# Half chunks: skipping the second half of a tile's last gathered chunk in four of five graph layers

## Chip, cores and metric

The kernel runs on one core of one Trainium2 chip. The metric is device time in microseconds (us) of one launch, and lower is better. TensorE multiplies matrices, VectorE (DVE in the rows) and ScalarE (ACT) work on elements, GpSimd (POOL) issues the indirect DMAs that gather and scatter rows of a table in memory, SyncE (SP) issues plain DMAs. Each engine runs an instruction stream of its own, and the streams meet at semaphores.

## The reference

A graph with 3125 nodes and 103125 directed edges (every node has an edge to itself) goes through four blocks, each followed by a layer norm of input plus output. Block 0 is attention over the incoming edges with 8 heads, block 1 a relational layer, block 2 two graph attention layers (GAT, 8 heads and then 1), block 3 a graph attention layer with 4 heads beside a selective scan over the nodes. All but block 1 have the same core; here is the one of block 2:

```python
e = jax.nn.leaky_relu(el[src] + er[dst], 0.2)
m = jax.ops.segment_max(e, dst, num_segments=n)
ex = jnp.exp(e - m[dst])
ssum = jax.ops.segment_sum(ex, dst, num_segments=n)
a = ex / ssum[dst]
rst = jax.ops.segment_sum(feat[src] * a[..., None], dst, num_segments=n)
```

For every edge the row `feat[src]` must be fetched, weighted and added to the row of its destination. A node has between 1 and 58 incoming edges.

## The kernel before

The nodes are sorted by their number of incoming edges, from most to fewest, and cut into T = 25 tiles of 128, one node per partition. A tile's edges are worked in **chunks** of S = 8 slots: slot s of a chunk holds for each of the 128 nodes the row of one neighbour (256 numbers and the heads' terms). So a tile needs as many chunks as its largest node fills: 8, 6, 6 for tiles 0 to 2, 5 for tiles 3 to 12, 4 for tiles 13 to 22, and 3 for the last two, 116 in a layer. A slot that a node doesn't fill carries an index beyond the table, which the gather leaves out, and an `extras` value that takes it out of the softmax. From the inputs, the largest nodes of tiles 0, 1, 2, 7 to 12 and 19 to 22 (13 tiles) fill at most the first four slots of their tile's last chunk.

`edge_softmax` works the layers conv (block 0), GAT 1 and GAT 2; `attend_and_scan` works the last one (its names begin with `m_`) with the selective scan on VectorE between its chunks. In all of them, per chunk:
1. SP (`load_record`) waits until buffer b has been gathered before, and loads the next 8 x 128 indices into `index[b]`; after `released[b]` it loads `extras[b]`.
2. POOL (`gather`) waits for the indices and for `released[b]`, and issues 8 indirect DMAs, one per slot, each adding 16 to the semaphore `gathered[b]`.
3. VectorE (`logits`) waits for `gathered[b]`, makes the logits and a running maximum; ScalarE takes the exponential; VectorE (`weigh`) multiplies rows and probabilities (L1100), which releases the buffer, and sums over slots, by itself in GAT and with TensorE in conv and the last layer.

Chunks alternate between the buffers b = 0 and b = 1 (a pair), and an odd last chunk has a third one, `TAIL_BUF`. In the last layer a tile's first two chunks have buffers of their own: `FIRST_BUF` and `SECOND`; there are four in all, and `SECOND` and the tail chunk take turns in one. The number of pairs is not known when the program is built: every engine reads words of a small table `sched` into registers at a tile's start (`Visit` in `edge_softmax`, `Stay` in `attend_and_scan`; a `value_load`), and the loop over pairs and the branch for the tail are done by registers. `fetch_nodes` makes the table once from the largest in-degree of each tile (`first`), by small VectorE operations on one partition. A tile's first two chunks are written out, with the previous tile's end (normalising, layer norm, scatter of its rows by POOL between the two gathers) woven in. The helper `new_steps` counts VectorE's finished operations: `st.do` appends one that waits for all before it.

What a wait compares with is worked out from the registers. Before, a chunk always adds 8 x 16:

```python
v.wait_ge(gathered[b], 16 + (u + 1) * 16 * S)
```

where `u = w.uses(a, b)` is how often buffer b has been used by then. The 16 comes from a small DMA that primes each semaphore.

Of the kernel before, what the change touches and what calls it, by code (L numbers as in the profile page):

```python
# [14 lines left out]
I32 = mybir.dt.int32  # L15
# [362 lines left out]
def fetch_nodes(nc, io, dr, kp, pr):  # L378


    with ExitStack() as ctx:
# [10 lines left out]
        more, cum_more, all_records = sb("f_more", [1, T]), sb("f_cummore", [1, T]), sb("f_allrecords", [1, T])  # L392
        has_more, long_tiles = sb("f_hasmore", [1, T]), sb("f_longtiles", [1, 1])
# [33 lines left out]
        def _(v):  # L427
# [27 lines left out]
            st.do(v.tensor_copy(kp["sched"][:, COUNT, 0:T], per[:, 0, :]))  # L455
            for k in (CHUNKS, RECORDS, USES):
# [345 lines left out]
CHUNKS, RECORDS, USES, COUNT, CODE, TAILS, LATER, LATER_CODE, MORE, MORE_AT, WORD = range(11)  # L802
# [6 lines left out]
TAIL_BUF = 2  # L809


class Visit:


    def __init__(self, eng, kp, t):
# [12 lines left out]
        self.chunks_end = self.chunks + count  # L828

# [8 lines left out]
FIRST_BUF, SECOND = 3, 4  # L838


class Stay:


    def __init__(self, eng, kp, t):
        def read(row, least, most):
            return eng.value_load(kp["sched"][0:1, row, bass.ds(t, 1)], min_val=least, max_val=most)
        code = read(LATER_CODE, 0, (CHUNKS_MAX // 2 << TAIL_BITS) + T)
        later = read(LATER, 0, E // S + 2)
# [4 lines left out]
        self.chunks = self.later + self.records + t  # L853

# [34 lines left out]
def visit(eng, kp, t, chunk, in_first=None):  # L889

    w = Visit(eng, kp, t)
# [12 lines left out]
    return w  # L904


def edge_layer(nc, io, dr, kp, layer):
# [10 lines left out]
    with ExitStack() as ctx:  # L918
# [60 lines left out]
        def _(sp):  # L979
# [8 lines left out]
            def load_record(w, a, b):  # L988
# [4 lines left out]
                sp.wait_ge(gathered[b], 16 + u * 16 * S)  # L993
# [6 lines left out]
            visit(sp, kp, 0, load_record)  # L1000
            with tile_loop(nc, sp, 1, T) as t:
                visit(sp, kp, t, load_record)

        @block.gpsimd
        def _(pool):
# [6 lines left out]
            def gather(w, a, b):  # L1012
# [7 lines left out]
                for s in range(S):  # L1020
# [3 lines left out]
                        bounds_check=limit, oob_is_err=False).then_inc(gathered[b], 16)  # L1024

# [20 lines left out]
            for t in range(2):  # L1046
                visit(pool, kp, t, gather)
            with tile_loop(nc, pool, 2, T) as t:
                visit(pool, kp, t, gather, first_pair(t - 2))
# [6 lines left out]
        def _(v):  # L1056
# [136 lines left out]
            def tile(t, first):  # L1193
                w = Visit(v, kp, t)
# [605 lines left out]
def attend_and_scan(nc, io, dr, kp):  # L1800
# [5 lines left out]
    with ExitStack() as ctx:  # L1806
# [82 lines left out]
        def _(sp):  # L1889
# [8 lines left out]
            def load_record(w, j, b):  # L1898
# [6 lines left out]
                sp.wait_ge(gathered[b], 16 + n * 16 * S)  # L1905
# [6 lines left out]
            with tile_loop(nc, sp, 0, T) as t:  # L1912
                w = Stay(sp, kp, t)
# [5 lines left out]
        def _(pool):  # L1919
# [5 lines left out]
            def gather(w, j, b):  # L1925
# [7 lines left out]
                for s in range(S):  # L1933
# [4 lines left out]

            with tile_loop(nc, pool, 0, T) as t:
                w = Stay(pool, kp, t)  # L1940
# [154 lines left out]
        def _(v):  # L2095
# [108 lines left out]
            def logits(st, w, j, b):  # L2204

                n = w.uses(j, b)
                v.wait_ge(gathered[b], 16 + (n + 1) * 16 * S)
# [38 lines left out]
            def tile(t, front, ahead, before):  # L2246
                w = Stay(v, kp, t)
# [280 lines left out]
def network(nc, io, result):  # L2528
# [17 lines left out]
    with ExitStack() as ctx:  # L2546
        def sb(name, shape, dt=F32):
# [5 lines left out]
            "inv_deg": sb("inv", [P, T]), "sched": sb("sched", [1, 11, 32], I32), "ident": sb("ident", [P, P]),  # L2553
# [55 lines left out]
```

## Time and profile before

| | us |
|---|---|
| median of 3 runs | 8107.87 (8107.5 to 8110.19) |
| the profiled execution's own time | 8107.49 |
| its span in the trace | 8105.7 |

| layer | from, to | chunks | gathers |
|---|---|---|---|
| conv | 430, 1810 | 116 | 928 |
| relational (not changed) | 1810, 3254 | 116 | 928 |
| GAT 1 | 3254, 4545 | 116 | 928 |
| GAT 2 | 4545, 5864 | 116 | 928 |
| last, with the scan | 5864, 7600 | 116 | 928 |

The share of busy time is an average over layers with different limits. In a timeline row, the number in brackets is the engine's idle time just before the instruction, and the name behind the arrow is what the trace holds for the event that ended it. An instruction on registers, a branch and a semaphore instruction are not counted as busy: they show as idle time, and the arrow then names whatever came last before.

### The profile page before, as it was taken

To read this page: it belongs to the slowest core of one execution; us is meant where nothing else is said; L and a number is where in the kernel's file an instruction comes from. 1 tells how busy PE (TensorE), PEld (TensorE's weight loads), DVE (VectorE), ACT (ScalarE), POOL (GpSimd) and SP (SyncE) were. 2 spreads that over 40 slices of the span, in tenths; PEclk is the share of its full clock that TensorE was granted. 3 is DMA by queue.
4 is the path that set the end of the run, shared out by engine and by line. 5 is a ranking of instruction groups with operands and counts; after the bars stand their busy time and mean duration, and the time that the engine had idled before them with its cause. 6 is when DMAs were issued, how large, how long until landed. Compare 5 with 4: busy or idle time off the path is not lost. (4 is left out here: it accounts for less than half of the span.)

```text
span 8105.7 us, 73810 instructions
## 1 busy us (share of the span) xinstructions
PE 3327.5 (41%) x15180; PEld 2657.1 (33%) x15181; DVE 5585.2 (69%) x11215; ACT 1258.9 (16%) x2734; POOL 5360.7 (66%) x4985
## 2 busy tenths in 40 slices
PE   3444544445667766112222100000155555555444
PEld 3233333334666666011111000000044444444333
DVE  7578888883333434788888677777767887777444
ACT  4101111110111111000000000010122232223111
POOL 0666766666777776777777677777667777776301
PEclk7767676777888888555555555555577777777666
DMA  2345555542332322333333233333233333332100
GB/s 82 91 133 166 166 156 165 157 125 82 89 86 82 88 84 59 88 95 92 91 100 88 59 91 94 87 96 91 71 92 107 108 104 101 107 99 81 51 6 9
DMA packets 489231, 773.98 MB, mean 95 GB/s; under 512 B 298796, under 2 KB 319767, under 8 KB 485436
## 3 DMA queue, kind: packets, MB, share of 16 engines
q0 software_dynamic: 265920, 667.09, 29.6%
q10 hardware_dynamic: 20536, 77.34, 2.5%
q1 hardware_dynamic: 202688, 28.69, 2.3%
q14 instruction: 68, 0.56, 0.0%
q8 instruction: 19, 0.31, 0.0%
HBM read 823.08 MB, written 46.52 MB: 107 GB/s over the span
## 5 line engine op out<-in xcount | busy, mean ns | idle before, releaser
L1021 POOL DMA_INDIRECT gat_rows<-scratch_gat,gat_index x1856 | 1858.3, 1001 | 583.7 <-issue 545.1
L1934 POOL DMA_INDIRECT m_rows<-scratch_gat,m_index x928 | 1219.7, 1314 | 507.0 <-issue 272.9
L1467 POOL DMA_INDIRECT rel_rows<-scratch_x,rel_index x928 | 1016.3, 1095 | 295.4 <-issue 281.8
L1021 POOL DMA_INDIRECT conv_rows<-scratch_kv,conv_index x928 | 931.5, 1004 | 420.8 <-issue 253.8
L1317 PE MATMUL conv_ps<-conv_work,k_ident 128*128 128x256 f32 x1856 | 680.9, 546 | 748.9 <-DVE conv_work L1100 678.2
L724 PE MATMUL gat_ps<-k_ident,gat_cur 128*128 128x128 f32 x100 | 34.4, 448 | 2127.9 <-DVEq L1184 1201.4
L1317 PEld LDWEIGHTS conv_ps<-conv_work,k_ident 128*128 128x128 f32 x1856 | 520.4, 287 | 909.8 <-issue 719.9
L724 PEld LDWEIGHTS gat_ps<-k_ident,gat_cur 128*128 128x128 f32 x100 | 14.4, 203 | 2163.5 <-DVEq L1184 1219.7
L1732 PE MATMUL rel_ps<-rel_factor,rel_rows 128*128 128x128 f32 x3712 | 595.8, 336 | 274.8 <-DMA rel_rows<-scratch_x,rel_index 274.3
L1732 PEld LDWEIGHTS rel_ps<-rel_factor,rel_rows 128*128 128x128 f32 x3712 | 577.9, 249 | 287.2 <-DMA rel_rows<-scratch_x,rel_index 183.7
L1112 DVE TENSOR_REDUCE gat_red<-gat_work 128x256 f32<-128x2048 f32 x182 | 652.2, 3583 | 0.0
L1100 DVE TENSOR_TENSOR gat_work<-gat_rows,gat_psprob 128x2048 f32<-128x2048 f32 x232 | 530.5, 2287 | 61.9 <-ACT gat_psprob L1252 50.4
L1990 PE MATMUL m_ps<-m_work,k_ident 128*128 128x256 f32 x1664 | 494.6, 466 | 171.4 <-DVE m_work L2224 171.4
L1990 PEld LDWEIGHTS m_ps<-m_work,k_ident 128*128 128x128 f32 x1664 | 392.6, 241 | 261.9 <-issue 190.0
L1974 PE MATMUL m_ps<-m_hs,k_ident 128*128 128x128 f32 x1600 | 278.8, 355 | 320.3 <-DVEq L2193 320.3
L1974 PEld LDWEIGHTS m_ps<-m_hs,k_ident 128*128 128x128 f32 x1600 | 269.3, 267 | 335.1 <-DVEq L2193 335.1
L1252 ACT ACTIVATE gat_psprob<-gat_logit 128x72 f32<-128x72 f32 (+1 forms) x232 | 48.2, 208 | 2129.9 <-DVE gat_logit L1092 2129.9
L2368 POOL DMA_INDIRECT out_x<-j_o,j_node x25 | 36.6, 1465 | 434.0 <-DVEq L2493 427.9
L1083 DVE TENSOR_TENSOR conv_dots<-conv_rows,conv_psown 128x2048 f32<-128x2048 f32 x116 | 265.3, 2287 | 83.5 <-DMA conv_rows<-scratch_kv,conv_index 37.7
L2224 DVE TENSOR_TENSOR m_work<-m_rows,m_ps 128x2048 f32<-128x2048 f32 x104 | 237.9, 2287 | 80.5 <-ACT m_ps L2056 80.5
L1100 DVE TENSOR_TENSOR conv_work<-conv_rows,conv_psprob 128x2048 f32<-128x2048 f32 x116 | 265.1, 2285 | 21.4 <-ACT conv_psprob L1252 20.4
L1084 DVE TENSOR_REDUCE conv_logit<-conv_dots 128x64 f32<-128x2048 f32 x116 | 265.1, 2286 | 4.0
(488 smaller groups left out, 7568.2 us busy)
## 6 DMA issues: line engine op xcount, KB each, us to landing
m_bc<-scratch_bc ACTq DMA_DIRECT2D x25, 2048.0 KB, 8.7
gat_rows<-scratch_gat,gat_index POOLq DMA_INDIRECT x1856
conv_rows<-scratch_kv,conv_index POOLq DMA_INDIRECT x928
rel_rows<-scratch_x,rel_index POOLq DMA_INDIRECT x928
m_rows<-scratch_gat,m_index POOLq DMA_INDIRECT x928
scratch_runs<-e_runs_sb ACTq DMA_DIRECT2D x1, 6453.1 KB
scratch_runs<-e_runs_sb SPq DMA_DIRECT2D x1, 6437.5 KB
scratch_kv<-p_row ACTq DMA_DIRECT2D x25, 256.0 KB, 2.5
```

What stands on the lines that cost most here:

```text
L1021: pool.indirect_dma_start(out=rows[b][:, s, :], out_offset=None, in_=table, in_offset=bass.IndirectOffsetOnAxis(ap=index[b][:, s:s + 1], a ...
L1083: st.do(v.tensor_tensor(dots[:], rows[b][:, :, 0:F], over_slots(own[:], S), ALU.mult))
L1084: st.do(v.tensor_reduce(lg, dots[:].rearrange(per_head, h=H), X, ALU.add))
L1100: v.tensor_tensor(work[b][:].rearrange(per_head, h=H), rows[b][:, :, values:values + F].rearrange(per_head, h=H), over_dims(prob[:, 0:S, : ...
L1112: st.add(v.tensor_reduce(red[:], slots, X, ALU.add))
L1317: ins = pe.matmul(ps_sum[min(b, 1)], ident, work[b][:, s, :], start=s == 0, stop=s == S - 1)
L1467: pool.indirect_dma_start(out=rows[b][:, g, :], out_offset=None, in_=dr["x1"], in_offset=bass.IndirectOffsetOnAxis(ap=index[b][:, g:g + 1] ...
L1732: ins = pe.matmul(ps_sums[h * 2 + g // 4][:, (g % 4) * P:(g % 4 + 1) * P], rows[b][:, g, h * P:(h + 1) * P], factor[b][:, g * BASES:(g + 1 ...
L1934: pool.indirect_dma_start(out=rows[b][:, s, :], out_offset=None, in_=dr["gat3"], in_offset=bass.IndirectOffsetOnAxis(ap=index[b][:, s:s + ...
L1974: ins = pe.matmul(ps_y[:, k, :], kp["ident"][:], hs[:, k, n, :], start=n == 0, stop=n == NS - 1)
L1990: ins = pe.matmul(ps_sum[bank_of(b)], kp["ident"][:], work[b][:, s, :], start=s == 0, stop=s == S - 1)
L2224: v.tensor_tensor(work[b].rearrange(per_head, h=H), rows[b][:, :, 0:F].rearrange(per_head, h=H), over_dims(prob[:, 0:S, :], D), ALU.mult). ...
```

## The change

`fetch_nodes` works out for each tile whether its last chunk is needed as a whole (the tile has three chunks or more, and its largest node fills more than `8 * count - 4` slots), and sums this up over the tiles before. The result is two new rows of `sched`, `WHOLE` and `LATER_WHOLE`, in one word per tile: the flag of this tile, how many tail chunks before were whole, how many b = 1 chunks before were whole. POOL gathers slots 4 to 7 of a b = 1 or tail chunk inside a branch on `whole_now`. Because a buffer's semaphore then no longer grows by 128 with each use, everyone who waits for it (SP in `load_record`, VectorE in `logits`) computes the value in halves of 64. In the relational layer `halves` stays off. What the skipped slots would have held stays in the buffer from an earlier chunk, and `extras` takes them out as before. VectorE still works on all eight slots.

```diff
@@ fetch_nodes
             st.do(v.tensor_copy(kp["sched"][:, COUNT, 0:T], per[:, 0, :]))
+            st.add(v.tensor_scalar(free[:], per[:, 0, :], float(S), float(-S // 2), ALU.mult, ALU.add))
+            st.add(v.tensor_scalar(half[:, 0, :], per[:, 0, :], 3.0, None, ALU.is_ge))
+            st.do(v.tensor_tensor(half[:, 1, :], per[:, 1, :], per[:, 2, :], ALU.subtract))
+            st.do(v.tensor_tensor(free[:], free[:], first[:], ALU.is_ge))
...
+            for k in range(2):
+                st.do(v.tensor_tensor_scan(wholes[:, k, :], whole[:, k, :], zero[:], 0.0, ALU.add, ALU.add))
+                st.do(v.tensor_tensor(wholes[:, k, :], wholes[:, k, :], whole[:, k, :], ALU.subtract))
...
+            st.add(v.tensor_copy(kp["sched"][:, WHOLE, 0:T], half[:, 0, :]))
+            st.do(v.scalar_tensor_tensor(half[:, 0, :], tile_no[:], -64.0, half[:, 0, :], ALU.mult, ALU.add))
+            st.do(v.tensor_scalar(kp["sched"][:, LATER_WHOLE, 0:T], half[:, 0, :], 64.0, None, ALU.add))
@@ new
+HALF = 16 * (S // 2)
+class Halves:
+    def read_halves(self, read, row, t):
+        word = read(row, t, 0, (CHUNKS_MAX // 2 << 6) + 63)
+        self.last_whole, self.whole_tails, self.whole_pairs = word & 1, (word >> 1) & 31, word >> 6
+
+    def whole_now(self, j, b):
+
+        if b == TAIL_BUF:
+            return self.last_whole
+        return (self.pairs > j + 1) | self.last_whole | self.tail
+
+    def landed_before(self, j, b):
+        if not self.halves or b not in (1, TAIL_BUF, SECOND):
+            return self.uses(j, b) * (2 * HALF)
+        return self.uses(j, b) * HALF + (self.whole_pairs + j if b == 1 else self.whole_tails + self.firsts(b)) * HALF
+
+    def landed(self, j, b):
+        if not self.halves or b not in (1, TAIL_BUF, SECOND):
+            return (self.uses(j, b) + 1) * (2 * HALF)
+        now = 1 if b == SECOND else self.whole_now(j, b)
+        return self.landed_before(j, b) + HALF + now * HALF
+
+def gather_slots(pool, w, j, b, one):
+    for s in range(S // 2):
+        one(s)
+    if b not in (1, TAIL_BUF):
+        for s in range(S // 2, S):
+            one(s)
+        return
+    with pool.If(w.whole_now(j, b) > 0):
+        for s in range(S // 2, S):
+            one(s)
@@ Visit and Stay, __init__
+        self.halves = halves
+        if halves:
+            self.read_halves(read, WHOLE, t)
@@ load_record, in both kinds of layer
-                sp.wait_ge(gathered[b], 16 + u * 16 * S)
+                sp.wait_ge(gathered[b], 16 + w.landed_before(a, b))
@@ gather, in both
-                for s in range(S):
+                def one(s):
                     pool.indirect_dma_start(
...
+                gather_slots(pool, w, a, b, one)
@@ logits, in both
-                v.wait_ge(gathered[b], 16 + (u + 1) * 16 * S)
+                v.wait_ge(gathered[b], 16 + w.landed(a, b))
@@ tile of edge_softmax
-                w = Visit(v, kp, t)
+                w = Visit(v, kp, t, halves=True)
```

How the engines' instruction lists change. `ISA` rows are register moves, address arithmetic or semaphore instructions, `TENSOR_LOAD` is a read of the table into a register. First VectorE in GAT 2, from the tile loop's head to the first operation on the first chunk. Before:

```order
L1237 ISA
L817 TENSOR_LOAD k_sched
L817 ISA x2
L68 ISA
L1196 MEMSET gat_top 128x1
L1197 ISA
L1197 COPY gat_own<-k_er 128x1
L1079 ISA
L1086 TENSOR_TENSOR gat_logit<-gat_rows,gat_own 128x8
```

And in the changed kernel:

```order
L1314 ISA
L881 TENSOR_LOAD k_sched
L881 ISA x3
L881 TENSOR_LOAD k_sched
L881 ISA x2
L68 ISA
L1273 MEMSET gat_top 128x1
L1274 ISA
L1274 COPY gat_own<-k_er 128x1
L1156 ISA
L1157 REGISTER_ALU
L1163 TENSOR_TENSOR gat_logit<-gat_rows,gat_own 128x8
```

There is a second read of the table, with three more `ISA` rows, ahead of the memset. Next VectorE in the same tile at its second chunk (b = 1), from the last operations of the previous tile's end to the first on the chunk. Before:

```order
L1163 COPY gat_node<-k_info 128x1
L755 RECIPROCAL gat_small<-gat_small 128x1
L756 TENSOR_SCALAR gat_cur<-gat_out,gat_small 128x256
L1086 TENSOR_TENSOR gat_logit<-gat_rows,gat_own 128x8
```

And in the changed kernel:

```order
L1240 COPY gat_node<-k_info 128x1
L776 RECIPROCAL gat_small<-gat_small 128x1
L777 TENSOR_SCALAR gat_cur<-gat_out,gat_small 128x256
L1156 ISA
L1156 REGISTER_ALU
L1156 ISA
L1156 REGISTER_ALU x4
L1156 ISA
L1163 TENSOR_TENSOR gat_logit<-gat_rows,gat_own 128x8
```

Eight instructions on registers now stand between the two operations, where there was none. Last POOL in GAT 2's loop over the remaining pairs and the tail chunk behind it. Before:

```order
L899 ISA
L1021 DMA gat_rows<-scratch_gat,gat_index 128x257 x16
L899 REGISTER_ALU
L899 COMPARE_AND_BRANCH
L898 UNCONDITIONAL_BRANCH
L902 REGISTER_ALU
L902 COMPARE_AND_BRANCH
L1015 REGISTER_ALU
L1015 ISA
L1021 DMA gat_rows<-scratch_gat,gat_index 128x257 x8
```

And in the changed kernel:

```order
L974 ISA
L1096 DMA gat_rows<-scratch_gat,gat_index 128x257 x12
L871 ISA
L871 REGISTER_ALU x2
L871 COMPARE_AND_BRANCH
L1096 DMA gat_rows<-scratch_gat,gat_index 128x257 x4
L871 UNCONDITIONAL_BRANCH
L974 REGISTER_ALU
L974 COMPARE_AND_BRANCH
```

The sixteen gathers of a pair are now twelve and, behind a compare and branch, four.

## Rows read from the trace of the kernel before

A page's group (rows 3) has: line, engine, operation, tiles, count, then busy us, mean ns of one, idle before and what ended most of it. A window (rows 2) has: from and to, length, then busy us and number of instructions of PE, PEld, DVE, ACT and POOL, then TensorE's granted clock as a share of full speed, the share of DMA time, GB/s. A timeline row has: start, duration, engine, line, operation, tiles, and the idle before in brackets. In rows 1 PE is TensorE's multiplying and PEld its loading of weights.

**Rows 1.** The page: busy time, share of the span and instructions of each engine.
```profile
PE 3327.5 (41%) x15180; PEld 2657.1 (33%) x15181; DVE 5585.2 (69%) x11215; ACT 1258.9 (16%) x2734; POOL 5360.7 (66%) x4985
```

**Rows 2.** The windows view: conv, GAT 1, GAT 2, last layer.
```profile
430.00:1810.00 1380.00, 666.43 (x1815) 509.49 (x1816) 1172.56 (x2113) 222.38 (x337) 955.17 (x951) 0.70 0.57 156
...
3254.00:4545.00 1291.00, 287.11 (x600) 160.83 (x600) 1035.92 (x2005) 66.26 (x244) 956.70 (x957) 0.52 0.34 88
4545.00:5864.00 1319.00, 72.56 (x159) 38.39 (x160) 1013.99 (x2102) 118.62 (x294) 981.40 (x982) 0.50 0.33 87
5864.00:7600.00 1736.00, 960.86 (x4199) 807.06 (x4198) 1320.36 (x2824) 488.77 (x1200) 1223.02 (x932) 0.76 0.33 97
```

**Rows 3.** The page's costliest groups: gathers of both GAT layers, and the last's.
```profile
L1021 POOL DMA_INDIRECT gat_rows<-scratch_gat,gat_index x1856 | 1858.3, 1001 | 583.7 <-issue 545.1
L1934 POOL DMA_INDIRECT m_rows<-scratch_gat,m_index x928 | 1219.7, 1314 | 507.0 <-issue 272.9
```

**Rows 4.** Timeline of POOL in GAT 2, one gather.
```profile
5098.49 0.99 POOL L1021 DMA_INDIRECT gat_rows<-scratch_gat,gat_index  x1 [0.30 <-issue]
```

**Rows 5.** Timeline of VectorE in GAT 2, tile 9 and the next memset.
```profile
5100.11 0.06 DVE L1196 MEMSET gat_top<- 128x1 f32 x1 [1.43 <-DVE gat_den L1127]
...
5101.33 0.17 DVE L1086 TENSOR_TENSOR gat_logit<-gat_rows,gat_own 128x8 f32<-128x8 f32 x1 [0.97 <-DMA gat_rows<-scratch_gat,gat_index]
...
5104.11 0.48 DVE L1155 SCALAR_TENSOR_TENSOR gat_out<-k_a,k_inv,gat_out 128x256 f32<-128x256 f32 x1 [0.17 <-DVE gat_out L1154]
...
5114.48 0.17 DVE L1086 TENSOR_TENSOR gat_logit<-gat_rows,gat_own 128x8 f32<-128x8 f32 x1 [0.79 <-DMA gat_rows<-scratch_gat,gat_index]
...
5124.90 0.17 DVE L1086 TENSOR_TENSOR gat_logit<-gat_rows,gat_own 128x8 f32<-128x8 f32 x1 [1.96 <-DMA gat_rows<-scratch_gat,gat_index]
...
5135.28 0.17 DVE L1086 TENSOR_TENSOR gat_logit<-gat_rows,gat_own 128x8 f32<-128x8 f32 x1 [1.92 <-DMA gat_rows<-scratch_gat,gat_index]
...
5145.00 0.17 DVE L1086 TENSOR_TENSOR gat_logit<-gat_rows,gat_own 128x8 f32<-128x8 f32 x1 [1.22 <-DMA gat_rows<-scratch_gat,gat_index]
...
5154.93 0.06 DVE L1196 MEMSET gat_top<- 128x1 f32 x1 [1.44 <-DVE gat_den L1127]
```

**Rows 6.** Timeline of VectorE in GAT 1: tile 9 (three rows), tile 20, tile 21's start.
```profile
3821.60 0.22 DVE L1086 TENSOR_TENSOR gat_logit<-gat_rows,gat_own 128x64 f32<-128x64 f32 x1 [1.32 <-DMA gat_rows<-scratch_gat,gat_index]
...
3832.01 0.23 DVE L1086 TENSOR_TENSOR gat_logit<-gat_rows,gat_own 128x64 f32<-128x64 f32 x1 [1.45 <-DMA gat_rows<-scratch_gat,gat_index]
...
3841.74 0.22 DVE L1086 TENSOR_TENSOR gat_logit<-gat_rows,gat_own 128x64 f32<-128x64 f32 x1 [0.76 <-DMA gat_rows<-scratch_gat,gat_index]
...
4328.22 0.23 DVE L1086 TENSOR_TENSOR gat_logit<-gat_rows,gat_own 128x64 f32<-128x64 f32 x1 [0.23 <-DVE gat_hid L1190]
...
4338.01 0.23 DVE L1086 TENSOR_TENSOR gat_logit<-gat_rows,gat_own 128x64 f32<-128x64 f32 x1 [0.83 <-DMA gat_rows<-scratch_gat,gat_index]
...
4347.70 0.23 DVE L1086 TENSOR_TENSOR gat_logit<-gat_rows,gat_own 128x64 f32<-128x64 f32 x1 [0.76 <-DMA gat_rows<-scratch_gat,gat_index]
...
4359.28 0.22 DVE L1086 TENSOR_TENSOR gat_logit<-gat_rows,gat_own 128x64 f32<-128x64 f32 x1 [0.45 <-DVE gat_own L1197]
```

**Rows 7.** Timelines in conv: POOL and VectorE in tile 9, VectorE in tile 16.
```profile
1039.46 1.00 POOL L1021 DMA_INDIRECT conv_rows<-scratch_kv,conv_index  x1 [5.30 <-DVE conv_work L1100]
...
1064.82 2.29 DVE L1083 TENSOR_TENSOR conv_dots<-conv_rows,conv_psown 128x2048 f32<-128x2048 f32 x1 [0.32 <-DVE conv_den L1127]
...
1421.97 2.29 DVE L1083 TENSOR_TENSOR conv_dots<-conv_rows,conv_psown 128x2048 f32<-128x2048 f32 x1 [0.82 <-DMA conv_rows<-scratch_kv,conv_index]
```

**Rows 8.** Timeline of VectorE in the last layer: a chunk of tile 1, the start of tile 10.
```profile
6058.32 0.19 DVE L2210 TENSOR_TENSOR m_logit<-m_rows,m_own 128x32 f32<-128x32 f32 x1 [5.62 <-DMA m_rows<-scratch_gat,m_index]
...
6641.64 0.06 DVE L2249 MEMSET m_den<- 128x4 f32 x1 [2.16 <-DMA gat_w_gat<-in_gat]
```

**Rows 9.** Timeline of VectorE in `fetch_nodes`, two operations.
```profile
266.85 0.17 DVE L454 TENSOR_TENSOR f_perf<-f_perf 1x25 f32<-1x25 f32 x1
267.05 0.17 DVE L455 CAST k_sched<-f_perf 1x25 int32<-1x25 f32 x1
```

More of the change, by code:

```diff
@@ L392, in fetch_nodes @@
         more, cum_more, all_records = sb("f_more", [1, T]), sb("f_cummore", [1, T]), sb("f_allrecords", [1, T])
+        free, half = sb("f_free", [1, T]), sb("f_half", [1, 3, T])
+        whole, wholes = sb("f_whole", [1, 2, T]), sb("f_wholes", [1, 2, T])
         has_more, long_tiles = sb("f_hasmore", [1, T]), sb("f_longtiles", [1, 1])
@@ L809, with __init__ @@
 TAIL_BUF = 2
-class Visit:
-    def __init__(self, eng, kp, t):
+FIRST_BUF, SECOND = 3, 4
+HALF = 16 * (S // 2)
+assert T < 32
+class Halves:
[25 more added lines that the diff above has]
+            one(s)
+class Visit(Halves):
+    def __init__(self, eng, kp, t, halves=False):
         def read(row, at, least, most):
@@ L835, in chunk, with __init__, read @@
         return self.chunks + j * 2 + (0 if b == TAIL_BUF else b)
[L838 to L848, printed above, removed]
+class Stay(Halves):
+    def __init__(self, eng, kp, t, halves=False):
+        def read(row, at, least, most):
+            return eng.value_load(kp["sched"][0:1, row, bass.ds(at, 1)], min_val=least, max_val=most)
+        code = read(LATER_CODE, t, 0, (CHUNKS_MAX // 2 << TAIL_BITS) + T)
+        later = read(LATER, t, 0, E // S + 2)
         self.t, self.later = t, code >> TAIL_BITS
@@ L853, in __init__, with firsts @@
         self.chunks = self.later + self.records + t
+        self.halves = halves
+        if halves:
+            self.read_halves(read, LATER_WHOLE, t)
+    def firsts(self, b):
+        return self.t + (1 if b == TAIL_BUF else 0)
     def uses(self, j, b):
@@ L886, in stay, with visit @@
         chunk(w, w.pairs, TAIL_BUF)
-def visit(eng, kp, t, chunk, in_first=None):
-    w = Visit(eng, kp, t)
+def visit(eng, kp, t, chunk, in_first=None, halves=False):
+    w = Visit(eng, kp, t, halves)
     if in_first is None:
@@ L1046, in _ @@
             for t in range(2):
-                visit(pool, kp, t, gather)
+                visit(pool, kp, t, gather, halves=True)
             with tile_loop(nc, pool, 2, T) as t:
-                visit(pool, kp, t, gather, first_pair(t - 2))
+                visit(pool, kp, t, gather, first_pair(t - 2), halves=True)
             if handed:
@@ L1912, in _ @@
             with tile_loop(nc, sp, 0, T) as t:
[L1913 removed]
+                w = Stay(sp, kp, t, halves=True)
                 load_record(w, 0, FIRST_BUF)
@@ L1932, in gather, with one @@
                 pool.sem_inc(pace, 1)
-                for s in range(S):
+                def one(s):
                     pool.indirect_dma_start(
@@ L1937, in gather @@
                         bounds_check=limit, oob_is_err=False).then_inc(gathered[b], 16)
+                gather_slots(pool, w, j, b, one)
             with tile_loop(nc, pool, 0, T) as t:
-                w = Stay(pool, kp, t)
+                w = Stay(pool, kp, t, halves=True)
                 gather(w, 0, FIRST_BUF)
@@ L2206, in logits @@
                 n = w.uses(j, b)
-                v.wait_ge(gathered[b], 16 + (n + 1) * 16 * S)
+                v.wait_ge(gathered[b], 16 + w.landed(j, b))
                 v.wait_ge(extras_in[b], (n + 1) * 16)
@@ L2246, in tile @@
             def tile(t, front, ahead, before):
-                w = Stay(v, kp, t)
+                w = Stay(v, kp, t, halves=True)
                 g = new_steps(v, g_steps)
```

21 lines of the change are left out of this document (16 added, 5 removed).

## Prediction

> **What bounds the kernel now.** I read the page first, then a table by stretch, then single tiles. The page [rows 1] names no bound: VectorE is busy for 69% of the span and GpSimd (POOL) for 66%. Cut at the layers [rows 2], the four layers that the change touches take 1380, 1291, 1319 and 1736 us, and VectorE and POOL lie close in each. POOL's busy time leaves out the gap behind every gather: in both GAT layers a gather takes 1001 ns and leaves (583.7 / 1856) = 0.31 us idle, "issue" for nearly all of it [rows 3]. So a gather costs 1.30 us (0.99 and the 0.30 ahead of it in [rows 4]), a chunk of eight 10.4, half a chunk 5.2. In the last layer a gather's mean is 1314 ns, half a chunk 5.3 with little idle.
>
> Then I asked in one middle tile of each layer who waits. The mark is VectorE's idle time before the first operation of each chunk, the wait for `gathered`. Part of it is no wait for data: the loop's and the address arithmetic's instructions, which aren't counted as busy. In tiles where VectorE is the later one, what is left is this floor: 1.43 before a tile's memset, 0.45 before the first chunk, 0.23 second, 0.83 at the loop's entry, 0.32 at its second chunk, about 0.75 before the tail [rows 5 to 7].
> - conv: VectorE. POOL waits 5.30 us per five-chunk tile for a buffer that VectorE releases; in four-chunk tiles VectorE waits a little itself (0.82 at the second chunk, about 0.8 over its floor) [rows 7].
> - gat2: POOL. A five-chunk tile takes 5154.93 − 5100.11 = 54.8 us, which is 42 POOL instructions (40 gathers, 2 scatters) at 1.305. VectorE idles above its floors for 0.52 + 0.56 + 1.13 + 1.60 + 0.47 = 4.3 us [rows 5]. A four-chunk tile: 34 × 1.305 = 44.4, slack 2.6 by the same reckoning (4.3 less one chunk's share, 1.7).
> - gat1: POOL, with little room. One scatter instead of two and eight heads instead of one: 41 × 1.305 = 53.5 us per five-chunk tile, slack 0.49 + 1.13 and next to nothing elsewhere = 1.65; 33 × 1.305 = 43.1 per four-chunk tile with slack 0.76 − 0.32 = 0.44 at its last chunk [rows 6].
> - last layer: VectorE, 1320 of 1736 us busy [rows 2], save in tiles 0 to 2, where chunks come gather by gather (idle 5.62) [rows 8], and the last two.
>
> **What the change takes away.** 13 of 25 tiles have a half-empty last chunk (0 to 2 and 7 to 12 with a tail chunk or b = 1, 19 to 22 with b = 1), so 52 gathers of 928 go in each of four layers, 208 × 1.30 = 270 us of POOL. Their slots carry an index beyond the table, so hardly a byte goes with them: the gain is POOL's instruction time only, and counts only where POOL is the later engine.
>
> **What it adds.**
> 1. VectorE. `landed` now needs a third word of the schedule and arithmetic with it, between one operation and the next. Is that hidden? The helper waits for the previous operation's semaphore before these instructions stand, so I say no. Witness: before L1155 one single such instruction stands, and 0.17 us are lost with nothing else to wait for [rows 5]. Prices: the loop's entry (0.83) has six register or branch instructions more than its second chunk (0.32), so 0.51 / 6 = 0.086 each [rows 6, 7]. The word: the memset of a tile idles 2.16 in the last layer, where two words are read ahead of it, and 1.44 in gat2, where one is [rows 5, 8]: 0.72 for a read with its address instructions. Counted in the instruction listing (its start stands with the change) per tile: the read 0.72; second chunk +8 → 0.70; loop entry −2 → −0.17; second chunk of the loop +4 → 0.35; tail chunk +1 or 2 → 0.13. Five chunks: 0.72 + 0.70 − 0.17 + 0.35 + 0.13 = **1.73 us**; four chunks (no tail, 0.09 less at the loop's end) **1.51**. Last layer by the same prices: 1.65 and 1.53. The Trainium skill speaks to the read, too: "DMA: Bandwidth & Descriptors", section "Latency and other measured facts", gives a floor of about 600 ns for a `tensor_load`. With that the four layers' 100 reads would cost up to 12 us less than by my row; the row's difference holds the address instructions as well, and I keep it.
> 2. POOL. One branch per b = 1 and tail chunk. The branches it has cost nothing visible: the gap stays at the 0.30 of [rows 4] over the loop's ends, since its sequencer is ahead. I take 0; bounds 0 and 0.51, the whole loop-entry surplus [rows 6, 7].
> 3. SP. Some eight instructions per record; SP has nothing else to do and stands at these very waits, on gathers or on VectorE's release, so the instructions come before a wait that is long anyway; I take 0. Should it be late, at 0.086 each it is 0.7 us of a chunk's lead.
> 4. `fetch_nodes`: 20 small operations in a row on one partition, 0.20 apart [rows 9]: +4.0 us, nothing beside it.
>
> **The sum, layer by layer.** A tile takes the longer of VectorE's time and POOL's.
> - conv: only cost. Ten five-chunk tiles 17.3; nine or ten four-chunk ones lose their 0.8 of slack first, 10 × (1.51 − 0.8) = 7; tiles 0 to 2 one, 23 and 24 two. **+27**. The halves give nothing: POOL waits anyway.
> - gat1: five-chunk tiles 1.73 − 1.65 = 0.1 each, 1; four-chunk ones 9 × (1.51 − 0.44) = 9.6; 23 and 24 2.4; first tiles 1. **+14**. Half a chunk less can't help, VectorE is the later one now.
> - gat2: VectorE's own tile is 54.8 − 4.3 + 1.73 = 52.2; POOL's with a half less 49.6. Gain 2.6 in six tiles, 15.4; tiles 19 to 22: 44.4 − (41.8 + 1.51) = 1.1, 4.3; tiles 0 to 2, where one half each shortens a POOL-bound stretch, about 6. POOL comes out of tiles 2 and 12 up to 5.2 ahead, and whole tiles behind spend that lead: 5 more in tiles 3 to 5, 5 in 13 to 16. With less than 1 at the end: **−34** (rounded down for the lead's loss).
> - last layer: 10 × 1.65 + 10 × 1.53 + 4.5 for tiles 0 to 2 + 2 = +38; gain in the gather-bound chunks of tiles 0 to 2, one half each, bounded by the idle there: 4.2 + 5.2 + 5.2 = 14.6. **+23**.
> - `fetch_nodes` **+4**.
>
> Sum +34. The profiled execution took 8107.49 us (span 8105.7), 0.4 under the median of 8107.87, so 8107.5 + 34 = 8141.5, by the median 8142, +0.42%. A measurement of this kernel tells about 0.2%, 16 us, from no change: 8092 and 8124 are the borders.
>
> **Rivals.**
> - *VectorE's sequencer runs ahead* (the other side). If the added instructions are done while an operation runs, all of 1 goes and the halves stand alone: gat1 −22, gat2 −50, last layer −15, conv 0, `fetch_nodes` +4: about −84, **8024**. For it: POOL's branches are hidden in just this way; against it: the 0.17 before L1155 and the 0.83 at the loop's entry [rows 5, 6]. It decides below roughly 70% of my prices, where the sum passes zero. The Trainium skill states the rule: "Advanced Engine Details and Errata", section "Sequencer Loop", lets other instructions be read and queued while a control instruction executes. By it alone the cost would vanish; the rows on VectorE speak against it here, since the operations wait for one another. Chance 0.08, with 0.04 for what lies between.
> - *Prices 20 to 30% lower*: an added move costs less than a branch, from which 0.086 comes. Costs of about 27 + 14 + 16 + 38 shrink by a quarter: **8110 to 8118**, within 0.2%. Chance 0.18.
> - *POOL's new branches show.* At 0.51 for each of 55 or so chunks per layer: nothing in conv and the last layer, +6 in gat1, +18 in gat2: **8166**. For it: after the branch the gathers must be fetched anew; against it the gaps at today's branches. Chance 0.12.
> - *It doesn't skip* (the flag is never zero): cost only, +27 +14 +38 +4, gat2 0, whose slack 4.3 covers 1.73: **8190**. The degrees say otherwise. Chance 0.03.
> - My forecast: 0.55, own range 8125 to 8160.
>
> **How the numbers follow.** Slower by over 0.2%: 0.55 + 0.12 + 0.03 = 0.70; same 0.18; faster 0.12. The range leaves out the two far cases and a part of the fourth: 8095 (prices at three quarters and gat2's gain full) to 8178 (branches and loads at their upper bounds).
>
> **What the trace after should show.** 876 gathers per layer instead of 928. The memset of a tile idles 2.15 instead of 1.44 in conv and the GAT layers, the second chunk 0.9 instead of 0.23 even where its data has long landed, `fetch_nodes` is 4 us longer. conv's five-chunk tile is 1.7 us longer, gat1's stays within 0.3 of 53.5, gat2's tiles 7 to 12 fall to 52.2 and are VectorE's. If the idle before the second chunk stays at 0.23, the first rival is true and the time is near 8024. If gaps of over 0.30 us stand at the fourth gather of a b = 1 chunk, it is the third. Most of the error will come from one price, that of a register instruction on VectorE: 10% of it and the read is about 8 us.

## The result and the profile after

The changed kernel takes 8181.09 us (median of 4 runs, 8179.9 to 8183.86), the kernel before 8109.03 beside it: 72 us or 0.9% slower, ratio 1.0088 with the interval 1.007 to 1.0105. The forecast was slower by 34 us, 8142, in a range that ended at 8178. The direction was right; the loss is twice the forecast one and lies just beyond the range.

The page after, its first section and the gathers of the GAT layers, as in [rows 1] and [rows 3]:

```profile
PE 3365.7 (41%) x15180; PEld 2683.0 (33%) x15181; DVE 5590.7 (68%) x11235; ACT 1258.8 (15%) x2734; POOL 5126.9 (63%) x4777
...
L1096 POOL DMA_INDIRECT gat_rows<-scratch_gat,gat_index x1752 | 1755.2, 1002 | 688.0 <-issue 498.8
```

POOL has 104 gathers less in the two GAT layers (1752 for 1856), each still 1.00 us, and its busy time fell by 234 us over the kernel. VectorE's busy time is the same within 6 us, and yet the span grew by 74: what was added on VectorE is idle time. TensorE is busy for 38 us more with as many instructions, 36 of them in the last layer, where its mean granted clock is 0.73 of full speed and was 0.76; VectorE doesn't wait longer for it (207 us from that layer's start on, before 218). The same windows as in [rows 2], moved to where the layers now lie (conv, GAT 1, GAT 2, last):

```profile
435.00:1852.00 1417.00, 667.88 (x1813) 511.59 (x1814) 1168.52 (x2112) 222.37 (x337) 901.89 (x899) 0.70 0.56 152
3297.00:4621.00 1324.00, 287.48 (x600) 161.17 (x600) 1039.41 (x2003) 66.27 (x244) 902.66 (x905) 0.51 0.33 86
4621.00:5921.00 1300.00, 72.68 (x159) 38.49 (x160) 1014.40 (x2102) 118.62 (x294) 932.47 (x930) 0.50 0.34 88
5921.00:7673.00 1752.00, 996.98 (x4199) 830.03 (x4197) 1318.63 (x2824) 488.73 (x1200) 1146.69 (x879) 0.73 0.33 96
```

conv 37 us longer, GAT 1 33, the last layer 16, GAT 2 19 shorter. Next to [rows 5], VectorE in GAT 2's tile 9 after the change (start, duration, ..., idle before; `remote` stands where the trace names no event that ended the idle time):

```profile
5168.87 0.06 DVE L1273 MEMSET gat_top<- 128x1 f32 x1 [2.13 <-remote]
...
5183.13 0.17 DVE L1163 TENSOR_TENSOR gat_logit<-gat_rows,gat_own 128x8 f32<-128x8 f32 x1 [1.17 <-issue]
...
5192.24 0.17 DVE L1163 TENSOR_TENSOR gat_logit<-gat_rows,gat_own 128x8 f32<-128x8 f32 x1 [0.67 <-DVE gat_den L1204]
...
5201.57 0.17 DVE L1163 TENSOR_TENSOR gat_logit<-gat_rows,gat_own 128x8 f32<-128x8 f32 x1 [0.89 <-DVE gat_den L1204]
...
5211.13 0.17 DVE L1163 TENSOR_TENSOR gat_logit<-gat_rows,gat_own 128x8 f32<-128x8 f32 x1 [1.11 <-DVE gat_den L1204]
...
5221.68 0.06 DVE L1273 MEMSET gat_top<- 128x1 f32 x1 [2.11 <-remote]
```

Before, the starts of this tile's chunks waited for their gathers, with up to 1.96 us of idle time; now none does. All of the idle time ahead of them is of the other kind: 2.13 ahead of the memset (1.43 before), 1.17 at the second chunk, 0.67 at the loop's entry, 0.89 at its second chunk, 1.11 at the tail. The tile takes 5221.68 − 5168.87 = 52.8 us, before 54.8. POOL, whose gathers of tiles 3 to 21 here all had 0.30 or 0.31 us ahead of them, now waits for a buffer in most tiles with a skipped half, and in conv more than twice as long as its 5.30 in [rows 7]:

```profile
5177.73 0.99 POOL L1096 DMA_INDIRECT gat_rows<-scratch_gat,gat_index  x1 [3.40 <-DVE gat_work L1177]
...
1059.42 0.99 POOL L1096 DMA_INDIRECT conv_rows<-scratch_kv,conv_index  x1 [12.07 <-DVE conv_work L1177]
```

The first row is GAT 2, the second conv, where the half that is not gathered only lengthens POOL's wait. GAT 1's tile 20, as in [rows 6]:

```profile
4384.10 0.23 DVE L1163 TENSOR_TENSOR gat_logit<-gat_rows,gat_own 128x64 f32<-128x64 f32 x1 [0.46 <-DVE gat_own L1274]
...
4397.08 0.23 DVE L1163 TENSOR_TENSOR gat_logit<-gat_rows,gat_own 128x64 f32<-128x64 f32 x1 [1.17 <-issue]
...
4406.71 0.23 DVE L1163 TENSOR_TENSOR gat_logit<-gat_rows,gat_own 128x64 f32<-128x64 f32 x1 [0.68 <-DVE gat_den L1204]
...
4416.54 0.23 DVE L1163 TENSOR_TENSOR gat_logit<-gat_rows,gat_own 128x64 f32<-128x64 f32 x1 [0.89 <-DVE gat_den L1204]
...
4428.80 0.23 DVE L1163 TENSOR_TENSOR gat_logit<-gat_rows,gat_own 128x64 f32<-128x64 f32 x1 [0.46 <-DVE gat_own L1274]
```

The idle times at its second, third and fourth chunk were 0.23, 0.83 and 0.76 and are 1.17, 0.68 and 0.89, and the tile is 4428.80 − 4384.10 = 44.7 us long for 43.0.

### The profile page after: what moved, and what is told of

The parts are those of the page before. It is cut to its first block and busy times, and to the rows that moved or that the text cites. A ratio compares the mean times of both kernels' runs of the same rounds, so it can differ in the third digit from the quotient of the medians.

```text
span 8179.4 us, 77034 instructions
## 1 busy us (share of the span) xinstructions
PE 3365.7 (41%) x15180; PEld 2683.0 (33%) x15181; DVE 5590.7 (68%) x11235; ACT 1258.8 (15%) x2734; POOL 5126.9 (63%) x4777
## 2 busy tenths in 40 slices
DMA packets 477585, 773.88 MB, mean 95 GB/s; under 512 B 287148, under 2 KB 308119, under 8 KB 473788
## 5 line engine op out<-in xcount | busy, mean ns | idle before, releaser
L1096 POOL DMA_INDIRECT gat_rows<-scratch_gat,gat_index x1752 | 1755.2, 1002 | 688.0 <-issue 498.8
L2011 POOL DMA_INDIRECT m_rows<-scratch_gat,m_index x876 | 1144.1, 1306 | 600.1 <-issue 255.9
L1096 POOL DMA_INDIRECT conv_rows<-scratch_kv,conv_index x876 | 878.3, 1003 | 511.9 <-DVE conv_work L1177 257.0
L745 PE MATMUL gat_ps<-k_ident,gat_cur 128*128 128x128 f32 x100 | 34.4, 448 | 2108.0 <-DVEq L1261 1171.4
L1160 DVE TENSOR_TENSOR conv_dots<-conv_rows,conv_psown 128x2048 f32<-128x2048 f32 x116 | 265.4, 2288 | 109.7 <-DVE conv_den L1204 33.3
```

Source lines behind the costliest of these rows:

```text
L1096: pool.indirect_dma_start(out=rows[b][:, s, :], out_offset=None, in_=table, in_offset=bass.IndirectOffsetOnAxis(ap=index[b][:, s:s + 1], a ...
L1160: st.do(v.tensor_tensor(dots[:], rows[b][:, :, 0:F], over_slots(own[:], S), ALU.mult))
L2011: pool.indirect_dma_start(out=rows[b][:, s, :], out_offset=None, in_=dr["gat3"], in_offset=bass.IndirectOffsetOnAxis(ap=index[b][:, s:s + ...
```

## The experiments

The first four kernels ran on a chip where the kernel before took 9293 us, not 8109, and then again on one where it took 8113; the readings rest on the second runs. Each ratio is to the kernel before on the same chip. The layer table that the readings rest on stands at the end of this section.

### The flag never set

The flag meant here is the one that lets a tile skip (`half` in `fetch_nodes`). No tile has 99 chunks, so none gets it, and every gather is issued.

```diff
-            st.add(v.tensor_scalar(half[:, 0, :], per[:, 0, :], 3.0, None, ALU.is_ge))
+            st.add(v.tensor_scalar(half[:, 0, :], per[:, 0, :], 99.0, None, ALU.is_ge))
```

First run:

> The changed kernel with the flag never set: every second half is gathered, while the reads, the register arithmetic before the waits, the branches and the new operations of fetch_nodes all stay. Only the costs are left. Theory A (my reckoning with prices corrected to the trace after: about 2.4 us of VectorE's register work per five-chunk tile, 2.1 per four-chunk tile, shown wherever VectorE is the later engine): conv +38, GAT 1 +33 to +36, GAT 2 0 to +3 because its slack of 4.3 covers 2.4, last layer +30, fetch_nodes +4.7, together about +108 to the kernel before, 8217. Theory B (the skipped halves themselves cost, by an uneven supply): about the time of the changed kernel, 8181, or less. Theory C (POOL's branches carry the cost): GAT 2, which POOL bounds, is slower by 15 or more.

9371.81 us against 9293.47, ratio 1.0082 (1.005 to 1.0114). Second run:

> [...] If the kernel before is near 8109 here, theory A expects 8217: conv +38, GAT 1 +33 to +36, GAT 2 0 to +3, last layer +30, fetch_nodes +4.7. Theory B (skipping itself costs): 8181 or less.

8221.78 us (8219.23 to 8226.01) against 8113.36, ratio 1.0137 (1.012 to 1.0153): +108 us. Theory A said 108, with prices taken from the trace after, so that the agreement bears out the split into costs and gain more than the prices. Skipping itself costs nothing: without it the kernel is 36 us slower still (108 for 72). The whole loss is in the bookkeeping and `fetch_nodes`, and the halves give back about a third of it. GAT 2 is back at POOL's pace, one tile from memset to memset:

```profile
5124.10 0.06 DVE L1273 MEMSET gat_top<- 128x1 f32 x1 [2.13 <-remote]
...
5179.09 0.06 DVE L1273 MEMSET gat_top<- 128x1 f32 x1 [2.13 <-remote]
```

55.0 us, as before the change (54.8), though the memset's idle is 2.13: there GAT 2's slack covers the bookkeeping, as forecast.

### The read alone

```diff
                 w = Visit(v, kp, t)
+                v.value_load(kp["sched"][0:1, TAILS, bass.ds(t, 1)], min_val=0, max_val=T)
```

and the same behind `Stay` in the last layer, on VectorE only, in the kernel before.

> The kernel before with one more read of the table into a register per tile on VectorE alone, in conv, both GAT layers and the last; nothing uses the value. Theory A: a tile's memset idles 0.70 us longer; conv's five-chunk tiles +7 in all, its four-chunk tiles nothing (slack 0.8), GAT 1's four-chunk tiles 0.26 each, GAT 2 nothing, the last layer 22 x 0.7 = 15: +22 to +28 in all, about 8133. Rival (the read is made ahead while VectorE works): within 5 us of before. If it is the main cost of the change: +60 or more.

9331.77 us against 9293.47, ratio 1.0035 (1.0016 to 1.0054).

> The extra read of the table on VectorE alone, again. Where the kernel before is near 8109: +22 to +28 us by theory A, within 5 us if the read is made ahead, +60 or more if it is the main cost.

8150.68 us against 8113.36, ratio 1.0048 (1.0032 to 1.0065): +37 us, 9 more than expected. The memset's idle in GAT 2, and in the last layer:

```profile
5116.78 0.06 DVE L1197 MEMSET gat_top<- 128x1 f32 x1 [2.17 <-remote]
...
6667.20 0.06 DVE L2251 MEMSET m_den<- 128x4 f32 x1 [2.86 <-DMA gat_w_gat<-in_gat]
```

2.17 for 1.43 and 2.86 for 2.16: 0.74 and 0.70 us per read, so the price of the forecast (0.72) was right. conv came as expected (+7). Beyond the expectation's terms are 5 us in GAT 1, 3 in GAT 2, and 6 in the last layer, where five-chunk tiles grew by 0.2 to 2.5 in turn. In the last layer VectorE's wait for TensorE ahead of `m_seq` (L1956) grew with it, from 11.3 to 17.1 us in all. In the four-chunk tiles there are such waits, too. Here are eight of these tiles (14 to 21, 518.1 us with the read alone, 511.4 before) in the waits view of VectorE (total us, times, longest):

```profile
DVE m_seq L2113 <- PE m_ps L1956: 8.8, 8, 1.2
DVE m_acc L2241 <- PE m_ps L1991: 6.6, 8, 0.9
DVE m_logit L2211 <- DVE m_hs L2193: 2.8, 8, 0.4
DVE m_logit L2211 <- DVE m_den L2245: 2.5, 8, 0.3
```

and the same tiles in the changed kernel (518.6 us), where `m_acc` has no such wait left:

```profile
DVE m_logit L2289 <- DVE m_den L2323: 9.2, 8, 1.1
DVE m_seq L2191 <- PE m_ps L2034: 6.7, 8, 0.9
DVE m_logit L2289 <- DVE m_hs L2271: 5.3, 8, 0.7
```

The arithmetic adds 9.2 us ahead of `m_logit`, and 8.7 us of waiting for TensorE go: here it costs next to nothing.

### POOL's part alone

The changed kernel with SP and VectorE waiting as before, POOL reading the word and branching, and the flag never set. An `Else` that is never taken stands behind the branch.

```diff
-            visit(sp, kp, 0, load_record, halves=True)
+            visit(sp, kp, 0, load_record)
...
-                w = Visit(v, kp, t, halves=True)
+                w = Visit(v, kp, t)
...
-                w = Stay(v, kp, t, halves=True)
+                w = Stay(v, kp, t)
```

> The kernel before with what the change puts on POOL alone, and never skipping: POOL reads the third word per tile and takes a branch before slots 4 to 7 of every b = 1 and tail chunk; fetch_nodes has its new operations; SP and VectorE wait as before. Theory A: POOL's sequencer is ahead of its gathers, so the branches cost nothing: +4 to +9, about 8115, nearly all of it fetch_nodes. Theory C (the branches show at up to 0.51 each): +18 in GAT 2, +6 in GAT 1, +30 or so in all.

9336.27 us against 9293.47, ratio 1.0052 (1.0032 to 1.0072).

> POOL's read and branches and fetch_nodes' operations alone, never skipping, again. Where the kernel before is near 8109: +4 to +9 us by theory A, +30 if the branches show. On the slower chip it was +0.52%, which would be 42 us here, with POOL waiting for indices there.

8119.62 us against 8113.36, ratio 1.0008 (0.9998 to 1.0018): +6 us, not clear of no change, and 3.8 of it ahead of conv. Two neighbouring gathers of GAT 2 in a stretch of forty:

```profile
5126.78 1.00 POOL L1098 DMA_INDIRECT gat_rows<-scratch_gat,gat_index  x1 [0.30 <-issue]
5128.08 1.00 POOL L1098 DMA_INDIRECT gat_rows<-scratch_gat,gat_index  x1 [0.30 <-issue]
```

Every gather of that stretch, across the branches too, has an idle time of 0.30 or 0.31 before it: POOL's branches are free. The first run's 0.52% is not explained by this; the last section comes back to that chip.

### Small DMAs in place of the skipped gathers

```diff
     with pool.If(w.whole_now(j, b) > 0):
         for s in range(S // 2, S):
             one(s)
+    with pool.Else():
+        for s in range(S // 2):
+            token(s)
```

where `token` is `pool.dma_start(spares[b][0:1, s:s + 1], dr["info"][0:1, 0:1]).then_inc(gathered[b], 16)`, with SP and VectorE as before.

> Skipping without any bookkeeping on VectorE and SP: where POOL skips slots 4 to 7 it issues four small DMAs of one word in their place, each adding 16 to the same semaphore, so that every use of a buffer adds 128 as before. A small DMA takes about 0.53 us of POOL instead of 1.30 (the four that prime the semaphores ahead of conv), so a skipped half saves 3.1 us instead of 5.2. Theory A: GAT 2 13 x 3.1 = -40, GAT 1 -15 to -20 (its slack bounds it), last layer -9, conv 0, fetch_nodes +4.7: about -60 to -65, 8045. If the cost of the change is not VectorE's bookkeeping: not faster than 8109. If the small DMAs cost as much as a gather: +5, 8115.

9040.62 us against 9293.47, ratio 0.9736 (0.9708 to 0.9764).

> Skipped gathers replaced by four small DMAs of one word, VectorE and SP as before, again. Where the kernel before is near 8109: 8045 by theory A (GAT 2 -40, GAT 1 -15 to -20, last layer -9, fetch_nodes +4.7); 2.6% as on the slower chip would be 7895, which this reckoning can't give.

8056.51 us (8055.76 to 8059.12) against 8113.36, ratio 0.9932 (0.9915 to 0.9948): −57 us, where −60 to −65 was expected. The small DMAs in the page's form (both GAT layers, last layer):

```profile
L1104 POOL DMA_DIRECT2D gat_spare<-scratch_info x104 | 55.3, 541 | 0.0
...
L2020 POOL DMA_DIRECT2D m_spare<-scratch_info x52 | 27.6, 538 | 0.0
```

0.54 us each, 2.1 for four, so a skipped half saves 3.1. GAT 1 gives 17 us, GAT 2 34, the last layer 7. The same halves are skipped as in the change, so without VectorE's and SP's bookkeeping the halves are worth more than they cost.

### The bookkeeping in another place

The values that VectorE's waits compare with are put into registers right behind the multiplication of an earlier chunk, and the word is read there too. `fetch_now` does this in a tile's first chunk, for the second chunk and the tail; `prepare` in each b = 0 chunk of the loop, for the one behind it. `regs` are registers allocated once per layer. SP's and POOL's part stays as in the change.

```diff
+    def prepare(self, eng, *chunks):
+        for j, b in chunks:
+            eng.reg_mov(self.regs[b], 16 + self.landed(j, b))
+            self.ready[b] = self.regs[b]
...
-                v.wait_ge(gathered[b], 16 + w.landed(a, b))
+                v.wait_ge(gathered[b], w.need(a, b))
...
                                 over_dims(prob[:, 0:S, :], D), ALU.mult).then_inc(released[b], 1)
+                if first:
+                    w.fetch_now(v, (0, 1), (w.pairs, TAIL_BUF))
+                elif b == 0:
+                    w.prepare(v, (a, 1))
```

> The changed kernel with VectorE's new work in another place: the third word is read, and the values that the waits compare with are moved into registers, right behind the multiplication L1100 of the chunk before (2.29 us long), instead of behind the semaphore of a finished operation. No instruction is taken away; two or three register moves per tile come on top. Theory A (the register work costs only where VectorE's sequencer stands behind its own last operation; the 102 us that the run with the flag never set showed beyond fetch_nodes are such work): all of it goes under that operation, only the gain of the halves and 4.7 us of fetch_nodes stay: GAT 1 -22, GAT 2 -50, last layer -14, about 8113 - 80 = 8033. Rival B (each such instruction costs its time wherever it stands): 8181 or slower. Rival C (the waits on a register's value cost, not the work for it): 8181 less the read, about 8145.

8021.08 us (8013.43 to 8024.89) against 8114.59, ratio 0.9886 (0.987 to 0.9903): −94 us, where the changed kernel has +72: 166 us better, with the same gathers and 54 more of VectorE's register instructions in the trace. Rivals B and C are out. VectorE in GAT 2's tile 9:

```profile
5055.94 0.06 DVE L1289 MEMSET gat_top<- 128x1 f32 x1 [1.40 <-DVE gat_den L1219]
...
5061.75 2.29 DVE L1188 TENSOR_TENSOR gat_work<-gat_rows,gat_psprob 128x2048 f32<-128x2048 f32 x1 [0.23 <-DVE gat_den L1301]
...
5069.29 0.17 DVE L1174 TENSOR_TENSOR gat_logit<-gat_rows,gat_own 128x8 f32<-128x8 f32 x1 [0.22 <-DVE gat_cur L777]
...
5078.39 0.17 DVE L1174 TENSOR_TENSOR gat_logit<-gat_rows,gat_own 128x8 f32<-128x8 f32 x1 [0.66 <-DVE gat_den L1219]
...
5087.29 0.17 DVE L1174 TENSOR_TENSOR gat_logit<-gat_rows,gat_own 128x8 f32<-128x8 f32 x1 [0.46 <-DMA gat_rows<-scratch_gat,gat_index]
...
5096.33 0.17 DVE L1174 TENSOR_TENSOR gat_logit<-gat_rows,gat_own 128x8 f32<-128x8 f32 x1 [0.57 <-DVE gat_den L1219]
...
5106.17 0.06 DVE L1289 MEMSET gat_top<- 128x1 f32 x1 [1.39 <-DVE gat_den L1219]
```

The idle times are those of the kernel before or less: 1.40, 0.22, 0.66, 0.46, 0.57. The tile takes 50.2 us, where the changed kernel's took 52.8 and the one before 54.8: VectorE's own 50.5 and nothing on it. The trace's records of the sequencer show where the work went: the read and the thirteen register and assert instructions with it lie between 5061.78 and 5063.82, all inside the multiplication L1188, which runs from 5061.75 to 5064.04. The 14 us beyond the expected −80 are mostly conv's, which is 11 us shorter though the halves are worth nothing there. About 4 of them are in its five-chunk tiles (58.2 for 58.6): part of the old arithmetic had moved as well, and tails start after 0.57 here, where the kernel before needs 0.75. The rest is spread over tiles 1 and 2, the four-chunk tiles and the relational layer, and was not traced to a cause.

> The same with the flag never set, so that every second half is gathered: by theory A the costs alone are those of fetch_nodes and POOL's branches, +6 us to the kernel before as in the run with these alone. Rival B: +108.

The same edit with the flag at 99.0. 8112.07 us against 8114.59, ratio 0.9997 (0.9987 to 1.0006). What cost 108 us costs nothing that this can tell, SP's and POOL's part included. So the place alone is worth 111 us with all gathers issued and 166 with the halves skipped: the other 55 are gain of the halves that the bookkeeping had used up.

> Only the read is moved under the multiplication, the arithmetic stays before the waits. Theory A: the changed kernel less what the read costs, of which the run with the read alone showed 37 us; a little less here since GAT 1's slack is used up by the arithmetic and so the read's 0.7 us in its 22 tiles comes off in full: 8181 - 40 to 50, 8135. Rival B: 8181.

Of the edit above only the read, with `prepare` empty. 8124.8 us against 8114.59, ratio 1.0014 (1.0005 to 1.0024): +10 us for +72, so 62 better than the changed kernel, where 40 to 50 was expected. The memset and the second chunk of GAT 2's tile 9:

```profile
5134.02 0.06 DVE L1288 MEMSET gat_top<- 128x1 f32 x1 [1.40 <-DVE gat_den L1218]
...
5148.28 0.17 DVE L1173 TENSOR_TENSOR gat_logit<-gat_rows,gat_own 128x8 f32<-128x8 f32 x1 [1.17 <-issue]
```

1.40 at the memset as before the change, 1.17 at the second chunk as after it: each piece of work shows at its own place. Moved first, the read is worth 62 us, and the arithmetic then the other 104 of the 166; the shares hold in this order only, since both use up the same slack (the read put into the kernel before cost 37).

### The change in GAT 2 alone

```diff
-            visit(sp, kp, 0, load_record, halves=True)
+            visit(sp, kp, 0, load_record, halves=layer == "gat2")
```

and so in all calls; `Stay` without halves, and `gather_slots` without the branch where `halves` is off.

> The change in GAT 2 alone; conv, GAT 1 and the last layer are as before. fetch_nodes +4.7, GAT 2 -20 to -23 (its slack covers the bookkeeping nearly, the halves shorten it): 8113 - 17 = 8096, 0.2% faster. If what GAT 2 gained in the changed kernel came from its later start or another layer: within 5 us of before.

8100.24 us against 8114.59, ratio 0.9982 (0.9972 to 0.9991): −14 us, where −17 was expected. GAT 2's −19 is its own.

### Where each layer stood

Microseconds from one layer's first operation on gathered rows to the next one's, as differences to the kernel before (443.2, 2823.2, 1290.8, 1328.9, 2219.6; starts in the traces, conv's share takes in the relational layer, the last one the end of the kernel):

| kernel | ahead of conv | conv | GAT 1 | GAT 2 | last | span |
|---|---|---|---|---|---|---|
| changed | +4.7 | +38.3 | +33.3 | −18.9 | +16.3 | +73.7 |
| flag never set | +2.9 | +39.5 | +34.4 | +4.4 | +30.6 | +111.8 |
| read alone | +0.2 | +7.4 | +6.9 | +2.9 | +21.2 | +38.6 |
| POOL's part alone | +3.8 | +1.8 | 0.0 | +1.1 | −0.1 | +6.6 |
| small DMAs | +2.5 | +4.5 | −17.3 | −33.8 | −7.0 | −51.1 |
| other place | +4.4 | −10.7 | −21.2 | −51.3 | −15.2 | −94.0 |
| other place, never set | +4.3 | −5.6 | +2.9 | +4.0 | +0.6 | +6.2 |
| read in another place | +3.9 | +26.7 | +14.3 | −29.8 | +2.1 | +17.2 |
| GAT 2 alone | +4.4 | +0.7 | +2.2 | −19.0 | +3.2 | −8.5 |

## Why the prediction was right in kind and half in size

Its steps one by one, by the table and the rows.

- **Who bounds each layer**: right. conv loses and gains nothing from the halves; the last layer gains only in its tiles 0, 1 and 2, which are 5.6, 3.9 and 3.6 us shorter than before (the forecast's 14.6 came to 14, the last layer of the changed kernel against that of the run with the flag never set), GAT 1 tips from POOL to VectorE, GAT 2 gains.
- **The price of VectorE's added instructions**: the step that failed. The mechanism was right: they are not hidden, they show ahead of the chunks. The read was sized right (0.72; measured 0.70 to 0.74) and needed no correction by the 12 us that the prediction held possible. The arithmetic was not: 0.086 per row of the listing gave +0.70 at the second chunk, +0.35 at the loop's second, +0.13 at the tail; measured were +0.94, +0.58 (0.89 for 0.31) and +0.36. Only the loop's entry came as said (−0.16). Together that is 1.7 us of arithmetic per five-chunk tile, where the sum had 1.0. In GAT 2 a five-chunk tile's bookkeeping is 2.4 us and not 1.73, a four-chunk tile's 2.0 to 2.1 and not 1.51. The one price was taken from moves and branches, and rows of one name in the listing are of different length: in the trace's records of the sequencer itself, ahead of GAT 2's second chunk in tile 9, the five simple operations take 40 to 53 ns and the three rows called ISA, each a fused group of register operations, 218, 110 and 120, with some 30 ns between neighbours. A divided total (0.51 over six) was carried to instructions of another kind.
- **conv +27**: +38. Five-chunk tiles grew by 2.3 us, where 1.73 stood, and four-chunk tiles by 1.2, where 0.7 was left after their slack.
- **GAT 1 +14**: +33. Here the error is leveraged: slack of 1.65 and 0.44 was to swallow nearly all of 1.73 and a third of 1.51, so that what comes on top counts in full. Five-chunk tiles grew by 1.0 us for 0.1, four-chunk ones by 1.7 for 1.1, and tiles 0 and 1, which the sum gave 1 us, by 4.5.
- **GAT 2 −34**: −19. VectorE's tile is 52.8, not 52.2, so tiles 8 to 12 give 1.9 to 2.0 each and not 2.6 (tile 7 nothing), the four-chunk ones about 0.5 and not 1.1, and the lead that POOL takes out of tiles 2 and 12 brings 2.8 us in tiles 3 and 4 and 2.6 in tiles 13 to 16, where 5 and 5 stood.
- **last layer +23**: +16. The cost is 31 and not 38, in spite of the higher price: five-chunk tiles grew by 1.75 us for 1.65, but four-chunk tiles (14 to 21) from 63.9 to 64.8 by the read alone and by no more with all of the bookkeeping. The sum gave this layer's tiles no slack; there was some, VectorE's wait for TensorE ahead of `m_acc` and `m_seq` (the rows under "The read alone"). Two errors ran against each other here, and that is luck.
- **fetch_nodes +4**: 2.5 to 4.7 ahead of conv, for 20 operations in 3.7 us.
- **POOL's branches 0, SP's instructions 0**: right (the run with POOL's part alone; for both, the moved bookkeeping with the flag never set, −0.03% with an interval that takes in 0).
- **Hardly a byte goes with the skipped gathers**: by the DMA packets, yes (773.88 MB for 773.98). The page's other count, of bytes read from memory, falls by 34.4 MB; what that one counts is told below.
- **The rivals.** That a quarter could come off the prices was given a chance of its own, that two fifths could come on top was not; the upper bound of the range took only the branches and loads and not the price that carried the sum. The first rival (the sequencer runs ahead) was told apart wrongly as a question of yes or no. The moved bookkeeping shows that it does run ahead, and where: the same work costs nothing measurable behind a 2.29 us multiplication, and some 100 us behind the semaphore step that ends each chunk, where the sequencer itself waits for VectorE's last operation (ahead of the second chunk of tile 9 the step's record stands at 5182.00, 0.04 us after that operation's end, and the first register row at 5182.10). The Trainium skill says in "Advanced Engine Details and Errata", section "Sequencer Loop", that an engine instruction is pushed into a queue and waits there for its semaphores, and that other engine instructions can be read and queued while a control instruction executes. The trace agrees with the first part: register instructions ran beside the multiplication in front of them. The second part, on which the first rival rested, no run here tests, since the operation behind the arithmetic waits for the value that it makes.

## What to carry to other kernels

Saving instructions on one engine pays only as far as the bookkeeping for it doesn't lengthen the other: here an estimated 270 us of gathers were taken off POOL and some 2 us per tile put on VectorE, which bounds three of four layers. Before pricing register work by a mean per row, look at what each row is and behind what it stands: put values for later waits into registers while a long operation runs, and not between the wait that ends one step and the first operation of the next. Slack turns an error of two fifths in the cost of a tile into a factor of two in the time.

## What was not expected of the hardware

- Register work costs by its kind and place: 40 to 53 ns for a simple operation, up to 218 for a fused group in the same stretch; about 0.94 us for eight rows where the sequencer had waited for its own engine, nothing measurable behind an operation in flight.
- A read of a word into a register costs 0.70 to 0.74 us of VectorE's idle time with what surrounds it, of which the read's own record is 0.30 to 0.31. The Trainium skill's floor of about 600 ns for a `tensor_load` ("DMA: Bandwidth & Descriptors", section "Latency and other measured facts") is not borne out by the record of the instruction alone.
- The page's count of bytes read from memory is not what the packets moved for indices beyond the table. It falls by 34.4 MB in all four layers and by 6.84 MB with the change in GAT 2 alone, which is just 52 gathers of 128 rows of 257 x 4 bytes, while the packets' bytes fall by 0.1 and 0.03 MB.
- The first four kernels ran where the kernel before takes 9293 us, 15% longer. VectorE's and POOL's instructions are as long there (a gather in the GAT layers 1.00 us), but the engines wait longer. One such wait is POOL's for its indices. In the GAT layers, the waits view (total us, times, longest) of the kernel with the read alone there:

```profile
POOL gat_rows L1021 <- DMA gat_index<-scratch_slots: 96.6, 20, 7.2
```

and of the same kernel where it takes 8151:

```profile
POOL gat_rows L1021 <- DMA gat_index<-scratch_slots: 21.7, 29, 7.3
```

That is four times as long for fewer waits, but only 75 of the 388 us that the two GAT layers take longer there, and the whole span is 1169 us longer. Plain DMAs as such are not shown to be slower: where that trace has all sixteen arrivals of a GAT index load (53 of 232), the last comes 1.68 us after the issue, as on the other chip; for the rest it can't be told. There the small DMAs gave 2.6% and not 0.7%, and POOL's part alone cost 0.5% and not 0.1%. Why, stays open.
